# Moving the shared expert's down product out of a fused attention and MoE kernel's tile loop

## The reference

```python
def reference(x, ctx, mask, ...):          # x: 4 x 1024 x 256, ctx: 4 x 77 x 256
    # cross attention, 16 heads of 16
    q, k, v = split_heads(layernorm(x)), split_heads(ctx), split_heads(ctx)
    attn = softmax(where(mask == 0, -1e9, q @ k.T / 4))
    x = x + (attn @ v) @ Wo.T + bo
    # mixture of experts on h = layernorm(x): 32 experts, 6 chosen out of 4 of 8 groups
    scores = sigmoid(h @ gate_w.T); sfc = scores + bias
    topk = top6(mask_groups(sfc, top4 groups by max))
    tw = scores[topk] / sum * 2.5
    routed = sum_e tw[e] * (silu(h @ gate_e.T) * (h @ up_e.T)) @ down_e.T
    # the shared expert, width 256: the part that the change is about
    sh = silu(h @ shared_gate.T) * (h @ shared_up.T)
    return x + routed + sh @ shared_down.T
```

## Time and profile before

| | |
|---|---|
| median of 3 runs | 800.1 us (798.34 to 802.43) |
| the profiled execution's own time | 801.02 us |
| its span, first to last instruction | 799.2 us |
| PE busy | 734.8 us, 92% |
| DVE busy | 522.0 us, 65% |
| ACT busy | 389.7 us, 49% |
| POOL busy | 535.6 us, 67% |

### The profile page before, as it was taken

One profiled execution on the slowest core, in us unless ns is written; L12 is line 12 of the kernel. 1 busy time (PEld: TensorE's weight loads), 2 busy tenths in 40 slices (PEclk: granted clock), 3 DMA queues, 4 the chain that ended last, 5 costly groups with the idle time before them and its releaser, 6 DMA issues.

```text
span 799.2 us, 18242 instructions
## 1 busy us (share of the span) xinstructions
PE 734.8 (92%) x5768; PEld 652.1 (82%) x5768; DVE 522.0 (65%) x1628; ACT 389.7 (49%) x832; POOL 535.6 (67%) x788
## 2 busy tenths in 40 slices
PE   6899999999999999986859999999999999999980
PEld 3789888888888888873449999998988999888970
DVE  4897777778777777665444425676775766566663
ACT  2455445444454445431026666666565666555550
POOL 0115788878787888877700007888888788987885
PEclk9899999999999999887879999999999999999995
DMA  9213443333344423432345557798888888878863
GB/s 272 94 54 100 126 133 120 120 115 131 119 133 126 134 100 126 138 120 100 107 159 170 173 167 231 243 279 248 262 261 257 252 263 250 257 239 253 259 214 108
DMA packets 97295, 140.13 MB, mean 175 GB/s; under 512 B 14944, under 2 KB 69732, under 8 KB 97201
## 3 DMA queue, kind: packets, MB, share of 16 engines
q1 hardware_dynamic: 77112, 87.50, 34.7%
q0 software_dynamic: 18432, 50.36, 20.3%
q10 hardware_dynamic: 1656, 1.10, 0.5%
HBM read 75.98 MB, written 62.94 MB: 174 GB/s over the span
## 4 chain that ended last, share of the span: by engine, by line
PE 36%; POOL 32%; issue 14%; DVE 8%; another core or an unknown queue 4%; DMA 2%; ACT 1%; DVEq 1%; POOLq 0%; ACTq 0%; SPq 0%
POOL rows L503 19%; PE sc_ps L994 19%; PE bank L1006 10%; POOL work L493 8%; PE sc_ps L978 4%; POOL work L541 2%; POOL rstd L513 2%; DVE firsts L1028 1%; DMA store<-in_x 1%; PE bank L898 1%; DMA work<-yrows,dest 1%; DVE work L1144 1%; DVE mx L1136 1%; PE sc_ps L885 1%
## 5 line engine op out<-in xcount | busy, mean ns | idle before, releaser
L994 PE MATMUL sc_ps<-work 128*128 128x128 f32 x1792 | 221.2, 277 | 5.9 <-DVE work L1491 2.9
L994 PEld LDWEIGHTS sc_ps<-work 128*128 128x128 f32 x1792 | 210.3, 193 | 8.7 <-issue 5.0
L541 POOL DMA_INDIRECT work<-yrows,dest x192 | 188.3, 981 | 35.6 <-POOL work L493 22.6
L503 POOL DMA_INDIRECT rows<-work,dest x192 | 187.7, 977 | 34.9 <-issue 34.8
L493 POOL MEMSET work<- 128x304 f32 (+1 forms) x360 | 136.6, 379 | 95.0 <-DMA yrows<-work 86.3
L1006 PE MATMUL bank<-wdn,work 128*128 x448 | 116.6, 383 | 5.3 <-DVE work L1446 3.3
L1446 DVE TENSOR_TENSOR work<-work,sc_ps 128x256 f32<-128x256 f32 x112 | 47.0, 419 | 113.3 <-ACT work L659 65.7
L1472 DVE SCALAR_TENSOR_TENSOR work<-work 128x256 f32<-128x256 f32 x160 | 76.9, 481 | 19.1 <-DMA work<-yrows,dest 12.7
L680 ACT ACTIVATE work<-bank 128x512 f32<-128x512 f32 x112 | 66.9, 597 | 45.5 <-PE bank L1006 25.7
L1006 PEld LDWEIGHTS bank<-wdn,work 128*128 128x128 f32 x448 | 76.5, 191 | 13.4 <-issue 7.6
L591 ACT ACTIVATE work<-work 128x1232 f32<-128x1232 f32 x32 | 39.4, 1231 | 91.1 <-DVE work L1144 81.7
(11 more groups left out here) (173 smaller groups left out, 1108.5 us busy)
## 6 DMA issues: line engine op xcount, KB each, us to landing
work<-rows SPq DMA_DIRECT2D x224, 128.0 KB
yrows<-work SPq DMA_DIRECT2D x112, 256.0 KB
wgu<-in_egu SPq DMA_DIRECT2D x16, 512.0 KB
store<-in_x SPq DMA_DIRECT2D x8, 512.0 KB, 12.0
wdn<-in_edn SPq DMA_DIRECT2D x8, 512.0 KB
rows<-padrow SPq DMA_DIRECT2D x8, 512.0 KB
out<-work SPq DMA_DIRECT2D x32, 128.0 KB
rows<-work,dest POOLq DMA_INDIRECT x192
```

Of the source, the lines that this page charges most:

```text
L503: pool.indirect_dma_start(rows[:, :], bass.IndirectOffsetOnAxis(ap=dest[:, t, k:k + 1], axis=0), rowb[:, m, :], None).then_inc(scat[m], 16)
L541: pool.indirect_dma_start(yg[:, g % RG, :], None, yrows[0:2 * n * P, :], bass.IndirectOffsetOnAxis(ap=dest[:, t, k:k + 1], axis=0)).then_i ...
L994: last = mm(ps8[2 + m % 2][:, (2 * w + g) * P:(2 * w + g + 1) * P], wst[w][m % 2][:, k * 2 * I + g * I:k * 2 * I + (g + 1) * I], xeT[:, m ...
```

## The change

All 32 tiles now go through `up`, `half_tanh` and `gated` in the loop. Only tiles 0 to 7 (`TS = 8`) keep `dn` and `add_shared` there. The down product of tiles 8 to 31 is made in 12 pairs by `late_down(p)` on PE (eight passes 256 wide each, in one of three banks of `sc_ps` in turn) and added to `x1` by `late_base(p)` on DVE. Pair 0 stands in PE's step 31, ahead of the last softmax's transposes (`tr_p(2)`), pairs 1 to 3 in steps 33 to 35, pair 4 behind the loop, 5 to 8 ahead of `lay_table`, 9 to 11 behind it. The 512 wide products are gone. Two more things move: in POOL's loop `inverse_std` of tile 31 now stands behind the first half of the scatter of tile 28 and not ahead of it, and DVE makes the mean and variance of `x1` ahead of `gated(1)` and `place_chosen`. The weights' reciprocal sums (`wnorm`) are made ahead of `name_blocks`. Since `x1` of 24 tiles is now kept, five of the eight loads of down weights come at the end or behind the loop and not four steps earlier.

```diff
-SE = 6
-TS = SE * B
+TS = 8
+NPL = (NT - TS) // 2
-NX = NT - B - TS
+NX = NT - TS
@@ PE
-                if 0 <= t - 5 < TS:
+                if t >= 5:
                     need(pe, "hidt", t - 5, 2)
                 if 0 <= t - 6 < TS:
                     need(pe, "sbase", t - 6)
@@
             def up(t, m, s):
-                if t >= TS:
-                    return
-                need(pe, "score_sub0", t + 4)
+                need(pe, "score_sub0", min(t + 4, NT - 1))
+                if t + 4 >= NT:
+                    need(pe, "hidt", t - 1, 2)
@@
+            def late_down(p):
+                t0 = TS + 2 * p
+                need(pe, "hidt", t0 + 1, 2)
+                if p < 3:
+                    need(pe, "score_sub", NT - 1)
+                else:
+                    need(pe, "base", p - 3)
+                for t in (t0, t0 + 1):
                     for k in range(KT):
+                        last = mm(late_ps(p)[:, (t - t0) * D:(t - t0 + 1) * D],
                                   store[:, t * D + k * P:t * D + (k + 1) * P], wsdn[:, k, :],
                                   start=k == 0, stop=k == KT - 1)
+                last.then_inc(S_["ldn"], 1)
@@
             count_chosen(NT - 2, NT)
+            late_down(4)
             number_blocks()
-            for s in range(SE + 1, SB + 1):
-                if s < SB:
-                    s_up(s, 0)
-                    s_up(s, 1)
-                if s == SE + 1:
+            for p in range(5, NPL):
+                if p == NPL - 3:
                     lay_table()
-                s_down(s - 1)
+                late_down(p)
@@ POOL
-                at_tile(tile, 0, inverse_std(NT - 1, NT))
                 at_tile(tile, 3, scatter(0))
-                at_tile(tile, 0, inverse_std(NT - 2, NT - 1))
+                at_tile(tile, 0, inverse_std(NT - 2, NT))
                 at_tile(tile, 3, scatter(1))
@@ DVE
+            def late_base(p):
+                t = TS + 2 * p
+                need(v, "ldn", p)
+                x1 = x1_pair(t)
+                tt(store[:, t * D:(t + 2) * D].rearrange("p (b d) -> p b d", b=2),
+                   late_ps(p).rearrange("p (b d) -> p b d", b=2), x1, ALU.add).then_inc(S_["base"], 1)
@@
             begin_blocks()
-            s_hidden(SE, 0)
+            late_base(3)
             follow_blocks()
-            s_hidden(SE, 1)
-            s_hidden(SE + 1, 0)
-            name_blocks()
-            read_table()
-            for s in range(SE + 1, SB + 1):
-                if s < SB:
-                    s_hidden(s, 1)
-                s_base(s - 1)
+            for p in range(4, NPL - 4):
+                late_base(p)
@@ (the four lines of wnorm stand here now)
+            name_blocks()
+            late_base(NPL - 4)
+            read_table()
+            for p in range(NPL - 3, NPL):
+                late_base(p)
```

More of the change, by code:

```diff
@@ L403, in _, with ld_behind @@
             over_tiles(step)
+            def ld_behind(i):
+                need(sp, "base", 2 * i + 1)
+                ld_down(E - NX + 4 * i)
+            ld_behind(0)
             need(sp, "tab", 0)
@@ L410, in _ @@
                          ).then_inc(S_["tab_ld"], 16)
+            for i in range(1, (NPL - 4) // 2):
+                ld_behind(i)
             sp.wait_ge(S_["table"], 2)
@@ L444, in _ @@
                 ld_tile(j)
-            for s in range(SE, SB - 1):
-                need(sp, "base", s - SE, 2)
-                ld_down(E - NX + 4 * (s - SE))
-            need(sp, "base", SB - 1 - SE, 2)
+            for i in range((NPL - 4) // 2, (NPL - 2) // 2):
+                ld_behind(i)
+            need(sp, "base", NPL - 1)
             ld_bc(2, bcA)
@@ L637, in _ @@
             over_tiles(step)
-            for s in range(SE, SB):
-                for h in range(2):
-                    a.wait_ge(S_["sg_ps"], 2 * (s - SE) + h + 1)
-                    if s > SE:
-                        a.wait_ge(S_["shh"], 4 * (s - SE - 1) + 2 * h + 2)
-                    a.activation(shg[:, h, :], ps8[2 * h], ACT.Tanh, scale=0.5).then_inc(S_["shg"], 1)
             for one in scat:
@@ L676, in ev_ye @@
                 if i == 0:
-                    need(a, "base", SB - 1 - SE, 2)
+                    need(a, "base", NPL - 1)
                 if i >= YP:
@@ L931, in step @@
                 at_tile(tile, -1, q_proj)
+                at_tile(tile, 4, late_downs)
                 at_tile(tile, 2, o_proj)
@@ L942, in step @@
                 at_tile(tile, 4, rank)
+                at_tile(tile, 0, late_first)
                 at_tile(tile, 0, tr_p(2))
@@ L1300, in step @@
                 at_tile(tile, 4, expert_top)
+                at_tile(tile, 4, late_bases)
             over_tiles(step)
@@ L1305, in _ @@
             v.memset(run[0:E, :, 0:NT], 0.0).then_inc(S_["sch"], 1)
-            def s_hidden(s, h):
-                done = 4 * (s - SE) + 2 * h
-                v.wait_ge(S_["shg"], 2 * (s - SE) + h + 1)
-                v.scalar_tensor_tensor(shg[:, h, :], shg[:, h, :], 1.0, ps8[2 * h], ALU.add, ALU.mult).then_inc(S_["shh"], 1)
-                v.wait_ge(S_["shh"], done + 1)
-                v.wait_ge(S_["sg_ps"], 2 * (s - SE) + 2)
-                mine = store[:, s * B * D:(s + 1) * B * D].rearrange("p (b k n) -> p k b n", b=B, k=KT)
-                v.scalar_tensor_tensor(mine[:, h, :, :], shg[:, h, :].rearrange("p (b n) -> p b n", b=B), 0.5,
-                                       ps8[2 * h + 1].rearrange("p (b n) -> p b n", b=B), ALU.mult,
-                                       ALU.mult).then_inc(S_["shh"], 1)
-            def s_base(s):
-                for half in range(2):
-                    t = s * B + 2 * half
-                    v.wait_ge(S_["sy_ps"], 2 * (s - SE) + half + 1)
-                    tt(store[:, t * D:(t + 2) * D].rearrange("p (b d) -> p b d", b=2),
-                       sy_ps[half].rearrange("p (b d) -> p b d", b=2), x1_pair(t), ALU.add).then_inc(S_["base"], 1)
             pos1, row, code, a_old, a_new = (tab[0:E, (1 + i) * NT:(2 + i) * NT] for i in range(5))
```

71 lines of the change are left out of this document (26 added, 45 removed).

## The result

| | before | after |
|---|---|---|
| median | 801.26 us (798.34 to 802.78, 4 runs) | 786.38 us (780.44 to 788.51, 4 runs) |
| ratio | | 0.9857, 95% interval 0.9815 to 0.9899 |
| profiled execution: own time, span | 801.02, 799.2 us | 788.51, 786.7 us |

What follows compares the result with a forecast made beforehand. PE was taken to bound the loop, POOL's scatters its end. First product 25.3 us earlier, less 2.5 for late hand-overs, gives 22.8: span 799.2 - 22.8 = 776.4, predicted 778 us (forecast 773 to 782, range 770 to 789).

Steps and rivals of the forecast that it cites:

- part 4: Table and sums behind the loop: last rank at DVE 365.3, table 381, `base` complete 386.7, first product at most 389.6.
- Part 1: Loop, tiles 13 to 28: without `dn` the step falls from 10.63 to 9.87 us, 11.4 us gained.
- The term for `dn`: PE's loop step: dropping `dn` takes off 0.87 us, from 10.63 to 9.76.
- The second bound: Loop step: the chain over the four banks of scores falls from 10.61 to 9.97 us.
- the middle of 9.76 and 9.97: Loop step taken as 9.87 us, between PE's own step and the chain over the banks.
- Part 2: Steps 28 to 30: each now has an `up` of 1.78 us; 29.6 us against 29.87, 0.3 gained.
- Part 3: POOL's scatters end at 383.2, 15.0 us earlier, with the 3.29 us variance wait filled; first product not before 390.0.
- Rival 1: Behind the loop: DVE waits for PE's signals behind ungapped scatters again, 8.2 us on the table; 783 us, chance 0.2.

Runs made afterwards that it cites:

- e12: The kernel before, unedited, run beside the changed one in a session whose traces show no hold: 783.6 us (1 run).
- e13: The changed kernel, unedited, in a session whose traces show no hold: 761.77 us, ratio 0.9792.
- e3: The changed kernel with `half_tanh` ahead of `exps` and the other work of its step on ACT: 787.04 us, ratio 0.9823.
- e7: The changed kernel with all scatters gapped and `inverse_std` of tile 31 back ahead of tile 28's first scatters: 786.6 us, ratio 0.9837.
- e8: The changed kernel, last 18 scatters without gaps, POOL waiting at each of the last three tiles until the previous tile's scatters landed: 787.83 us, ratio 0.9815.
- e1: The changed kernel with a short memset (gap) ahead of every scatter, the last three tiles' too: 779.98 us, ratio 0.9766.
- e4: The kernel before with every scatter gapped: 796.81 us, ratio 0.9962.
- e5: The changed kernel with only the six scatters of tile 31 left without a gap: 783.56 us, ratio 0.9783.
- e6: The changed kernel with the scatters of the last eight tiles without gaps: 791.44 us, ratio 0.9888.
- e16: The changed kernel with the counts of tiles 0 to 28 made two steps earlier, ahead of the scatters without gap: 759.88 us, ratio 0.9751.
- e17: The edit of e16 once more on the changed kernel, in another session: 760.8 us, ratio 0.9767.
- e2: The changed kernel with the 30 early count products moved from ahead of the last rank product to behind the loop: 797.81 us, ratio 0.9996.
- e14: The edit of e1 once more, every scatter of the changed kernel gapped, in a session without hold: 765.57 us, ratio 0.9836.

## Why the prediction was right in direction and wrong in size

Worked out from the rows above and those of before, the way from `qk` of tile 13 to the first expert product in its two pieces:

| us | before | after | change | e12 | e13 | change | predicted change |
|---|---|---|---|---|---|---|---|
| `qk` 13 to `qk` 31 | 189.4 | 179.2 | -10.2 | 186.7 | 174.8 | -11.9 | -11.7 |
| `qk` 31 to first product | 75.9 | 73.5 | -2.4 | 65.3 | 62.5 | -2.8 | -11.1 |
| of these, to the last rank at DVE | 37.2 | 49.2 | +12.0 | 32.1 | 35.4 | +3.3 | +0.4 |
| of these, scatters' end to first product | 17.1 | 16.3 | -0.8 | 7.7 | 8.5 | +0.7 | -7.8 |

**The step that failed** is in part 4: "taken off: 2.3 of the 2.60 us that DVE waits there without a cause that the row names", and with it the table at 381, which took off the 8.23 us as well. These 10.5 us (9.4 of them hold) are nearly all of the 11.1 that the end was to gain. In the result they were not removed but moved: the last rank now falls into a row of 12 scatters without gap, is held 11.55 us, and DVE was there at 375.03 and not at 365.3, which is 49.2 us after `qk` of tile 31 and not 37.6. In sessions 3 and 4 they were never there, so that they could not be gained. With the rank so late it is the path through DVE, and not the scatters, that sets the start in after. Either way the end gives 2.4 to 2.8 us. (By the medians after gains 20.9 and 16.8 us in these two sessions, near the 22.8 forecast; but the profiles of e12 and e13 have 14.7 us of it on the way to the first product, 11.9 of them in the loop.) The path was otherwise well laid: with no hold, e13 has the rank 35.4 us after `qk` of tile 31 (predicted 37.6), the table 50.8 (53.3), the first product 62.5 (64.8).

**Part 1, the loop.** Right in what it gains. Step 9.98 where 9.87 was predicted, 9.8 us gained and not 11.4. The term for `dn` was exact: in session 4, where PE waits for nothing, the step falls from 10.58 to 9.71, by the 0.87 it was costed at. The second bound, the chain of 9.97 us over the banks, was not one: the same code takes 9.71 there. In the result the step was longer by 0.27; e3 took PE's waits for `gated` away and came to 9.83, and the rest goes with the hold's sessions. That the middle of 9.76 and 9.97 came so near to 9.98 is partly luck.

**Part 2.** 29.5 us against 29.6. The 1.78 us for a narrow `up` held. Eight of them at two and a half times the price, as the Trainium skill's figures would have had it (TensorE: Matmul & The Clock Gate, section Back-to-back issue gap), were not seen with the fp32 operands of this kernel.

**Part 3, the scatters.** Their end at 383.06 against 383.2. That is luck: start-up was 3.35 us shorter, and POOL lost 3.19 us waiting for the held rank's places. The gain of POOL's new order is shown by e7 (4.4 us) and by e12 against e13 (scatters' end 57.6 and 54.0 us after `qk` of tile 31, 3.5 where 3.3 was said). Its tail was too short: 8.5 us from the last scatter's end to the first product in e13, not 6.8, since a landing takes longer than 1.6 (e8).

**Rival 1**, DVE waiting behind the ungapped scatters once more, is what happened. It put the wait at the table and 783 us; it stood at the rank, where it costs more because less runs beside it. Its chance of 0.2 was too small. The argument against it, that other signals in that stretch came at once, was weak: they were in part signals of DVE and ACT, and those are held in no trace. Two waits that no row explains had the same neighbour, and that was reason enough to let both return.

**What was not touched.** The expert stage took 387.4 us in the profile of after and 384.0 before, while the traces with the hold, e1 to e8, spread from 382.7 to 389.5 for the same code of that stage; with start-up (145.9 to 153.6) this makes a single profile uncertain by several us, and only the pieces between marks can be read to 1 us.

**What stays open.** What holds PE's signals. The runs show where it strikes: POOL must be issuing indirect DMAs (no late signal between 383 and 466 us of after, and the rank just behind a pause of POOL passes in e8), gaps shorten it (e1, e4, e5), and scatters without gap in more steps bring it to more places (e6). Theory P, POOL alone holds them until it stops, fails to explain ACT's 375.49 and PE's groups of three in e6, and the rank of e8. Theory Q, completions of PE that pass on slowly, fits these and the three signals that arrive together in after, but it is only argued, since e16 and e17 met no hold. Its second half, that the short products are the backlog, is not needed: the table of before was held 7.1 us with none of them near, and the last `up` is held ahead of them in after and e6. Since the profile models the ends of PE's rows, the traces can't tell a product that finishes late from a signal that travels late. The hold is not a property of the chip (session 2 against session 6). What was different between the sessions is not shown; the missing records go with it in all nineteen traces, so that the recording itself is a rival that no run tested. That the 20 us between the two levels are this hold is argued too: the end of the loop has 10.6 us of it in before (75.9 - 65.3) and 11.0 in after (73.5 - 62.5), the loop 2.7 and 4.4, and the expert stage 9.1 and 10.5 us (384.0 and 387.4 less 374.9 in e12 and 376.9 in e13), with PE at 96 of 100 us and not 100. The sums, 22 and 26, are about the distance of the levels.

## What to carry to other kernels

A wait for which no row has a cause must be kept in the sum when work is moved: ask what was going on beside it, and put it where the moved hand-over will meet the same neighbour. Cost the path once with the wait and once without, and predict between them. Where an edit pays in one session and costs in another, as the gaps here (ratio 0.9766 with them and 0.9857 without when signals are held, 0.9836 and 0.9792 when they aren't, the latter two within each other's intervals but 3.3 us apart in the profiles), more than one session has to decide before it is kept.

## What the runs showed of the hardware

- One program has two levels, 2.6 to 2.9% apart, with the same mean duration of the expert products' rows (276 ns in after, 277 in e13): 801 us for the kernel before in the result and in sessions 1 and 2, 779 to 781 in sessions 3 to 6, and both on one chip. The clock granted over the whole run hardly differs (0.971 and 0.978 for after); in the 33 us from 28.8 us after `qk` of tile 31 on it does, 0.74 against 0.99, and there PE had been idle for 8.23 us in the first and for no more than 2.67 in the second.
- A hold of up to 20 us (e2) between the end of PE's row and the moment its semaphore is raised, while POOL issues indirect DMAs, in ten traces of nineteen. The signals of DVE and ACT are not held in them.
- Scatters of 0.96 us without gap come every 1.26 us (374.86 - 362.22 for ten in e6), gapped ones every 1.48; the gap costs POOL 0.22 us each, 4 us for 18, and e14 is slower than e13 by 3.8.
